# A graph layer with edge sums on one core: an eleventh range of counted edges, the close of node quads in bursts, and two banks for the last sums

## The reference, cut to what matters

```python
x = x + gnn(layernorm(x), src, dst, eps, W1, b1, W2, b2, gamma, beta)
x = x + ffn(layernorm(x)[None], gate_w, gate_b, w1, b1, w2, b2)[0]   # 8 experts, top 1

def gnn(h, src, dst, ...):
    neigh = segment_sum(h[src], dst)                 # 200000 rows of 256 values
    h = relu(((1 + eps) * h + neigh) @ W1 + b1) @ W2 + b2
    return (h - mean) * rsqrt(var + 1e-5) * gamma + beta   # mean, var over all nodes
```

## Time and profile before

| what | us |
|---|---|
| median of 3 runs (2704.42 to 2734.87) | 2713.54 |
| the profiled execution, whole | 2722.03 |
| its span, first to last instruction | 2720.3 |
| norm stage and plan, up to the first gather | 118.5 |
| groups 0 to 110 gathered | 118.5 to 1506.4 |
| groups 111 to 135 gathered | 1508.9 to 1844.3 |
| last sum, last two quads | to 1889 |
| routing and experts | 1891 to 2720 |

### The profile page before, as it was taken

How to read it: one execution, slowest core, us unless ns; L and a number is a source line. 1 busy time by engine, 2 the same in 40 slices (tenths; PEclk the granted TensorE clock), 3 DMA queues, 4 the chain that set the end, 5 groups by cost and what they waited for, 6 DMA issues and landing times. The chain is left out here.

```text
span 2720.3 us, 35963 instructions
## 1 busy us (share of the span) xinstructions
PE 1843.1 (68%) x9315; PEld 1055.5 (39%) x9316; DVE 1386.2 (51%) x4375; ACT 911.7 (34%) x1518; POOL 1553.5 (57%) x1530
## 2 busy tenths in 40 slices
PE   0035456767858878676787765557764888979996
PEld 0012223333424444333343433334332555646664
DVE  8834544545544443334342322223664676858886
ACT  6811012323323333223221110102553555545553
POOL 1266665665565666556565654650445566847775
PEclk9966678888779889889898877788887999989998
DMA  7653335656658766575677422421662322140220
GB/s 228 226 186 106 108 86 178 206 187 193 222 181 264 241 201 203 189 232 192 211 250 252 137 79 69 128 82 58 212 196 87 101 81 79 34 144 22 92 89 21
DMA packets 228639, 411.91 MB, mean 151 GB/s; under 512 B 46469, under 2 KB 110299, under 8 KB 228406
## 3 DMA queue, kind: packets, MB, share of 16 engines
q1 hardware_dynamic: 164742, 243.58, 27.4%
q0 software_dynamic: 61520, 164.41, 19.8%
q10 hardware_dynamic: 2144, 1.05, 0.1%
HBM read 338.06 MB, written 75.06 MB: 152 GB/s over the span
## 5 line engine op out<-in xcount | busy, mean ns | idle before, releaser
L948 POOL DMA_INDIRECT space<-table,space x1083 | 1036.6, 957 | 719.4 <-issue 310.2
L1043 PE MATMUL e_sums<-space 128*128 128x256 f16 x1728 | 258.3, 314 | 175.5 <-DVE space L1327 168.9
L2007 POOL TENSOR_TENSOR space<-space 128x512 f16<-128x512 f32 x200 | 296.8, 1510 | 105.3 <-ACT space L2141 100.8
L1316 DVE SCALAR_TENSOR_TENSOR space<-e_sums,above,space 128x256 f32 x141 | 68.2, 484 | 553.4 <-remote 391.5
L1043 PEld LDWEIGHTS e_sums<-space 128*128 128x128 f16 x1728 | 194.7, 113 | 239.4 <-issue 189.4
L1117 PE MATMUL e_up<-e_hT,edge_weights 128*128 128x512 f32 x384 | 211.9, 688 | 88.4 <-ACT e_hT L1218 57.3
L2097 PE MATMUL x_down<-space 128*128 128x256 f16 x2208 | 250.7, 276 | 15.9 <-DVE space L2234 15.6
L2073 PE MATMUL x_up<-space 128*128 128x512 f16 (+1 forms) x1200 | 253.1, 371 | 2.9 <-ACT space L2141 2.9
L1212 ACT ACTIVATE space<-e_tally 128x392 f32 (+1 forms) x193 | 104.9, 543 | 447.7 <-PE e_tally L1082 144.4
L2141 ACT ACTIVATE space<-x_up,b_two 128x512 f32<-128x512 f32 (+1 forms) x400 | 248.6, 691 | 17.3 <-PE x_up L2073 11.8
L1082 PE MATMUL e_tally<-w2f 128*128 128x490 f16 x343 | 136.3, 472 | 161.7 <-DVE w2f L1371 121.7
(11 more groups left out here) (230 smaller groups left out, 2522.3 us busy)
## 6 DMA issues: line engine op xcount, KB each, us to landing
w1f<-table SPq DMA_DIRECT2D x490, 256.0 KB
counts<-in_x SPq DMA_DIRECT2D x48, 512.0 KB, 4.6
space<-table,space POOLq DMA_INDIRECT x1083
slot_rows<-space SPq DMA_DIRECT2D x64, 268.0 KB
space<-slot_rows SPq DMA_DIRECT2D x32, 536.0 KB, 7.3
table<-space SPq DMA_DIRECT2D x25, 512.0 KB, 3.0
out<-space SPq DMA_DIRECT2D x24, 512.0 KB
w1f<-in_w SPq DMA_DIRECT2D x8, 1024.0 KB, 5.2
```

The source lines that it names most:

```text
L948: pool.indirect_dma_start(got[:, r, t, :], None, table.rearrange("p h d -> (p h) d"), bass.IndirectOffsetOnAxis(ap=idx[:, h, first + t:fir ...
L1043: ins = nc.tensor.matmul(sums[:, 0, 0:D], hot[:, place, t, :], got[:, r, t, half * D:(half + 1) * D], start=(t == 0 and half == 0), stop=( ...
L2007: nc.gpsimd.tensor_tensor(midl[:, j % 2, c, :], midf[:, c % MB, :], midh[:, j % 2, c, :], ALU.subtract).then_inc(s_mlo, 1)
```

## The change

It is one change of the plan with what that needs of memory.

- `UNITS` gets an eleventh range of 24 tiles: 504 counted tiles, so 133 gathered groups instead of 136. The windows of the groups from 108 on are 30 instead of 33. The tests of the plan hold for this `dst` as before.
- The range count is odd now, so `FILLED` is 0 and counting starts in slot 0 (before: slot 3). The group limits move with it.
- Until all ranges are spread, a slot gets one quarter (two if more than two quads wait, before: two or three). After that it gets four when a quad waits, else three. `CLOSE`, `TENSOR_ROOM` and `BACK` are moved to fit.
- `e_sums` has two banks, used in turn by the windows of the looped part. The second is also `product`, so all ranges must be spread before slot `SINGLE`. The sum of a window waits only for the add before the last one.
- Small tensors of the norm stage (`n_ok`, `n_first`, ...) lie in a free part of `counts`.

The planner then gives: tiles in slots 0 to 99, pieces in slots 20 to 106, the last spread in slot 107. 112 quarters lie in slots 0 to 107 and 80 from 108 on. Ten quads are turned from slot 108 on: in slots 108, 110, 112, 114, 116 and 118 (each with four quarters and then four, but for slot 118), then 121, 124, 127 and 131. 54 slots hold eight pieces, 2 of them without a quarter.

```diff
-UNITS = (152, 64, 50, 41, 36, 32, 29, 27, 26, 23)
+UNITS = (152, 64, 50, 41, 36, 32, 29, 27, 26, 24, 23)
-GROUPS = ((96, 4, 5), (168, 2, 5), (WIDE, 1, 5), (HT, 1, 7))
+GROUPS = ((96, 4, 5), (176, 2, 5), (WIDE, 1, 5), (HT, 1, 7))
-CLOSE = {3: 20, 4: 29, 5: 38, 6: 45, 7: 53, 8: 59, 9: 66, 10: 72, 11: 78, 12: 83, 13: 89, 14: 94, 15: 99, 16: 104,
-         17: 108, 18: 113, 19: 117, 20: 122, 21: 126, 22: 130, 23: 134}
-TENSOR_ROOM, VECTOR_ROOM, BEHIND = 1120, 960, 300
-BACK, LENT_FROM, LENT = 105, 18, QT * D * 13 // 2
+CLOSE = {3: 17, 4: 26, 5: 35, 6: 43, 7: 50, 8: 56, 9: 63, 10: 69, 11: 75, 12: 80, 13: 86, 14: 91, 15: 96, 16: 101,
+         17: 106, 18: 110, 19: 115, 20: 119, 21: 123, 22: 127, 23: 131}
+TENSOR_ROOM, VECTOR_ROOM, BEHIND = 1080, 960, 300
+BACK, LENT_FROM, LENT = 102, 18, QT * D * 13 // 2
...
-            n = H1C if slot >= NG - 1 else 3 if waiting or spread == NU or len(quarters) > 2 * (due - slot) else 2
+            n = H1C if slot >= NG - 1 or spread == NU and len(waiting) > 0 else 3 if spread == NU else 2 if len(waiting) > 2 else 1
...
-                    self.quarters[slot], quarters = [None, *quarters[:2]], quarters[2:]
+                    n = n if spread == NU and len(waiting) > 0 else min(n, 2)
+                    self.quarters[slot], quarters = [None, *quarters[:n]], quarters[n:]
...
-assert sorted(ORDER) == list(range(NQ)) and max(SLOTS_OF.spread) < NG - 2 and max(SLOTS_OF.turn) == NG - 2
+assert sorted(ORDER) == list(range(NQ)) and max(SLOTS_OF.spread) < SINGLE and max(SLOTS_OF.turn) == NG - 2
...
-        sums = psum("e_sums", [P, 1, 2 * D], F32)
+        sums = psum("e_sums", [P, 2, 2 * D], F32)
-        product = psum("e_product", [P, 2 * D], F32)[:, :]
+        product = sums[:, 1, :]
...
-                        pe.wait_ge(s_add, turn)
+                        pe.wait_ge(s_add, pe.snap(pe.snap(turn) - 1))
-                                ins = nc.tensor.matmul(sums[:, 0, 0:D], hot[:, place, t, :],
+                                ins = nc.tensor.matmul(sums[:, place, 0:D], hot[:, place, t, :],
...
-                            out=row, in0=sums[:, 0, 0:D], scalar=mask[:, group], in1=row,
+                            out=row, in0=sums[:, place, 0:D], scalar=mask[:, group], in1=row,
...
-                        add_window(group_no(dve.snap(last_group))).then_inc(s_add, 1)
+                        add_window(group_no(dve.snap(last_group)), dve.snap(1 - place)).then_inc(s_add, 1)
```

More of the change, by code:

```diff
@@ L694, in words @@
                 also(nc.vector.tensor_scalar(plan.cols[:, :], gmini, ok[:, 0:1], None, ALU.mult))
-                also(nc.vector.tensor_scalar(plan.above[:, :], blocki[:, 1, :], place[:, 0:1], 1.0 / X_SCALE, ALU.is_le,
+                also(nc.vector.tensor_scalar(plan.above[:, :], blocki[1], place[:, 0:1], 1.0 / X_SCALE, ALU.is_le,
                                              ALU.mult))
@@ L1310, in _, with add_window @@
                 flushed = [0]
-                def add_window(group):
+                def add_window(group, place=0):
                     for b, mask in ((0, plan.above), (1, plan.below)):
@@ L1443, in _ @@
                 dve.wait_ge(s_add, dve.snap(dve.snap(turn) - 1))
-                then(add_window(group_no(dve.snap(last_group))))
+                then(add_window(group_no(dve.snap(last_group)), dve.snap(dve.snap(dve.snap(turn) + 1) % 2)))
                 for slot in LATE:
```

33 lines of the change are left out of this document (17 added, 16 removed).

## The result

The change made the kernel slower. Its median is 2808.8 us (2783.7 to 2846.8) against 2721.8 (2704.4 to 2734.9) in the same comparison, a ratio of 1.029 with a 95% interval of 1.023 to 1.036. I had predicted 2689 us with a range of 2656 to 2722. The execution of 2846.8 us is in a slower state than the others and does not enter the ratio.

What follows compares the result with a forecast made beforehand. No engine is full; the limit is GpSimd's gather rhythm with waits for earlier sums. The terms -36.9 + 0 + 0.5 + 13.7 - 2 give -24.7 us, 2689 us against the median of 2713.5; range 2656 to 2722.

Steps and rivals of the forecast that it cites:

- the eleventh range on TensorE: Slots 0 to 107: 49 us of added matmuls hidden by the gather rhythm; 0, ends -29 and +8 us.
- the rival of the pieces: Early slots with eight pieces: two more long gaps behind table loads, +16 us, 2705 us; chance 0.17.
- The even plan: Early part and turns: fewer overfull slots save 20 us, packed pairs are seldom held, 7 more; 2662 us; chance 0.22.
- Three groups less: Late part: 24 gathers and three slots go, at the bare pace of 12.3 us each; -36.9 us.
- the late one: Sign of being right: the late part from group 111 to 132 takes 285 to 320 us.
- the early one: Sign of being right: group 3 to 110 takes 1330 to 1360 us.
- The denser end: From slot 108 on: longer packed pairs of slots +6.5 us, more held turns +7.2; +13.7 us, ends 0 and +74.
- The end bound by TensorE: From slot 108 on: further turns held at 9.65 us each; 2749 us with all ten held; chance 0.15.
- One-hots: VectorE: 15 us more of one-hots, hidden in idle time but slowing the gathers slightly; +0.5 us.
- Two banks: Last windows: TensorE no longer waits for the add before; -2 us, ends -7 and 0.
- The clock: Late packed pairs: by the clock rule fuller slots stay warm, making the sum 4.5 us lower.
- bare group: Gather rhythm: eight gathers and a gap of 2.5 to 2.7 us, 12.3 us from group to group.

Runs made afterwards that it cites:

- experiment 14: The changed kernel as it is, run again on another chip of the 2700 us kind: 2814.7 us, 1.033 of the kernel before.
- experiment 2: The kernel before with all pieces and then all tiles of a slot in one share, on a 2300 us kind of chip: 2502.6 us, ratio 1.089.
- shares kept: The changed kernel with pieces and tiles handed out in three shares in every slot: 2705.9 us, 0.995 of the kernel before, on a 2700 us kind of chip.
- seven pieces: The changed kernel with three shares in every slot and at most seven pieces a slot instead of eight: 2695.1 us, ratio 0.990, on a 2700 us kind of chip.
- experiment 7: The changed kernel with three shares in every slot and one bank for the last sums: 2341.4 us, ratio 1.018, on a 2300 us kind of chip.

## Why the prediction was wrong

**The group numbers.** The prediction's pace has a slip: 848 gathers are 106 groups, so the stretch in the earlier trace rows ends with the first gather of group 109, and that at 1508.92 belongs to group 110 (so in the table of times, too, the first stretch is groups 0 to 109 and the second 110 to 135). The pace before was 1345.32 / 106 = 12.69 us early and 331.92 / 25 = 13.28 late, an excess over 12.3 of 41 and 24 us instead of 29 and 37. It shifts weight from the late to the early part and would have moved the sum by little.

**The failed step is "the eleventh range on TensorE: 0, ends -29 and +8".** It measured +110.8 us in the profiled execution, and +138 in that of experiment 14 (1495.7 - 1357.6). I wrote that "13 quarters leave the same slots" and that "the new plan is more even", and in the rival of the pieces that "the quarter in nearly every one of these slots now covers a load". I priced the quarters that move as TensorE time alone. But the number of quarters in a slot is also the number of shares into which its pieces and tiles are cut. One quarter where there were none or two turned three or two shares into one. This could be read before any run, from `parts_of` and `share` and from the plan's 44 such slots. The trace of before could not show it: its one slot with eight pieces and one part (slot 102) has no tiles, so that there is nothing to alternate. It kept the next group 18.7 us away, against 13.4 behind the other 37 slots of eight pieces, but four slots of the old plan with three parts kept it 19.9 to 21.2 us away, and on the chip of experiment 2 slot 102 took 11.0. With the shares kept the step measured 1370.1 - 1357.6 = +12.5 us, some 13 more by the median of that kernel, and with seven pieces -3.7. So as a price of the range alone, on this kind of chip, 0 and the upper end of +8 were somewhat low; on the other kind the range costs 54.5 us or more.

**The rival of the pieces** (2705 us, +16) had the right place, full slots whose sums come late behind table loads, and named the sign that came true: more than five gaps over 8 us, of which there are 12. Its price was a seventh of what happened, since it counted more full slots of the old kind and not slots of a new kind. **The even plan** (2662) did not occur as the change was written; the seven pieces version is nearest to it, 28.8 us under before where this rival had 51.5.

**Three groups less: -36.9** was right to a few us. Of the signs I had named, the late one was missed narrowly (285 to 320 us; it was 283.6, and 273.6 if the first gather is taken at group 111 as counted here) and the early one by far (1330 to 1360; it was 1468.4). The late part from the first gather of group 110 to that of the last group went from 331.9 us in 25 groups to 283.6 in 22, which is 48.3 us; at the old late pace three groups are 39.8. On the faster kind of chip the whole late stretch won 31.9, for 3 x 10.0.

**The denser end: +13.7** had the wrong sign in this execution: the 49.6 us that the late part won are 11.5 more than three groups at 12.3 us and the 1.2 us of the banks. Of ten turns from slot 108 on, two were held, for 9.3 and 11.3 us from transposes to products (in slots 116 and 121), not 3.75. The hold of the earlier trace rows is there, and the same turn can be held in one kernel and go through in another. That this depends on where it falls against the gathers, as the prediction said, fits but was not tested:

```profile
1514.33 1.06 PE L1109 MATMUL e_up<-ident,space 128*128 128x128 f32 x8 [2.36 <-remote]
1525.01 5.24 PE L1120 MATMUL e_up<-e_hT,edge_weights 128*128 128x512 f32 x6 [9.61 <-issue]
```

This is slot 108 of the kernel with seven pieces, held for 10.7 us; in the changed kernel the same turn took 2.2. The stretch from group 110 to the last add took 305 to 341 us over ten executions with the same late plan on this kind of chip, with up to four turns over 10 us. The longest of them, 340.5, belongs to four such turns, the shortest, 304.7, has none. So the term's size, 7.2 us for holds, is within what varies from one early part to the next, and +6.5 for the pairs is not to be seen: the turns that are not held take 2.2 to 3.1 us, most of them less than the 3.05 that I had put in. **The end bound by TensorE** (2749) was a rival on the right side of the result for the wrong reason: the end won 49.6 us.

**One-hots: +0.5.** A gather took 961 instead of 957 ns, which is 4 x 857 = 3.4 us for the early part. The Trainium skill (SBUF — State Buffer, the part on the port pair that VectorE and GpSimd share) says that fast VectorE copies lock GpSimd out while they run; by that rule the whole 15 us of one-hots could have been added, as an estimate, and the trace shows 3.4.

**Two banks: -2** fits in sign and nearly in size. From the last gather's end to the last add it was 24.9 us before and 23.7 after. The rows of TensorE that answer to the earlier trace rows show the wait for the add gone, and a shorter one for the next one-hots in its place:

```profile
1918.71 2.83 PE L1063 MATMUL e_sums<-space 128*128 128x256 f16 x16 [3.05 <-DVE space L1353]
1922.04 2.35 PE L1063 MATMUL e_sums<-space 128*128 128x256 f16 x16 [0.49 <-DVE space L1353]
```

L1353 makes one-hots, L1318 adds; the first of the two waits is longer than any before, and it is why the gain is small. With one bank experiment 7 showed no difference either.

**The clock.** In the three lumped slots the granted clock is 0.74, in the same slots with three shares 1.00, and that is 13 us of longer matmuls in 57. I had weighed the clock for the late part only, at 4.5 us. In slot 56 above it is 1.00, which is 2.4 GHz, from 888.8 to 895.5 us, where TensorE is busy for 4.79 us and has the wait of 1.83, and 0.50, which is 1.2 GHz, from 895.6 to 909.1, where it is busy for 11.03 us, before it rises again. The Trainium skill (TensorE: Matmul & The Clock Gate, Part 1) says that the array runs at 1.2 GHz after idle time and at 2.4 GHz once it has been busy; the trace agrees with these two changes.

In sum: on this kind of chip the change with shares kept (2705.9 against 2723.9, or -18; by the ratio -13) would have been within the range around the forecast of -24.7 us, which for its size is luck in part: the late part won more than its terms and the early part lost what they had at 0. The change as written added about 109 us to that (2814.7 - 2705.9).

## What to carry to other kernels

Where a helper cuts work by the length of a list, changing the list for any other reason changes the cut. When a diff changes how many items of one kind go into a step, read the functions that use this count, also those that the diff leaves alone. A step of before that already has the new count is a hint only if it also has the work that the count divides; here the one such slot had no tiles. Work that waits on a handshake of banks and work that waits on a ring of loads should alternate: in a block each shows its waits, and the matmuls around them ran slower, which here was the larger part of the price. The gain of a saved iteration is to be held against the pace of the chip that runs it.

## What the runs showed of the hardware

**Two kinds of chip.** I had not expected that the same kernel takes 2298 us on one chip and 2722 on another. The gathers take the same time on both (0.95 us, 1.25 apart). What differs is when a finished sum is seen while they run. The kernel before on the chip of the prediction, GpSimd's gathers, TensorE's sum and VectorE's add:

```profile
875.30 1.91 PE L1043 MATMUL e_sums<-space 128*128 128x256 f16 x16
876.33 0.94 POOL L948 DMA_INDIRECT space<-table,space  x1 [0.30 <-issue]
877.58 0.95 POOL L948 DMA_INDIRECT space<-table,space  x1 [0.30 <-issue]
880.60 0.48 DVE L1316 SCALAR_TENSOR_TENSOR space<-e_sums,above,space 128x256 f32 x1 [4.23 <-remote]
...
881.18 0.95 POOL L948 DMA_INDIRECT space<-table,space  x1 [2.66 <-remote]
```

And the kernel before with three shares on a chip of the other kind:

```profile
877.61 1.91 PE L1044 MATMUL e_sums<-space 128*128 128x256 f16 x16
877.94 0.94 POOL L949 DMA_INDIRECT space<-table,space  x1 [0.30 <-issue]
879.19 0.95 POOL L949 DMA_INDIRECT space<-table,space  x1 [0.30 <-issue]
879.70 0.48 DVE L1317 SCALAR_TENSOR_TENSOR space<-e_sums,above,space 128x256 f32 x1 [0.65 <-PE e_sums L1044]
...
880.44 0.95 POOL L949 DMA_INDIRECT space<-table,space  x1 [0.30 <-issue]
```

In the first the sum ends at 877.21, the eighth gather at 878.53, and the add starts at 880.60: 3.4 us after the sum and 2.1 after the gather. In the second the sum ends at 879.52 and the add starts 0.18 us later, in the middle of the gathers. Over slots 4 to 107, of 66 sums that ended while gathers ran 60 were seen more than 1.2 us late in the first, at the median 1.9 us after the eighth gather's end; in the second 10 of 92 were, and the median delay is 0.18 us. That is the gap of 2.6 us between groups, which I had taken as a fixed part of the bare group. The hold of the turns is probably the same thing; the rows show only that it occurs on the same kind of chip. From group 3 to the last add the kernel before takes 1717.9 us on the one kind and with three shares 1372.6 on the other, which is 345 of the 409 us between the two spans. No turn from slot 108 on was held on the faster kind. What holds the signals there the rows don't say.

**A load's pace and the lump.** With loads of half the size the lumped slots keep the next group 14.03 us away instead of 15.78 and 16.18, and the interleaved ones 12.99 and 13.13 instead of 13.50. The 14.03 is of the execution that is 28 us under its median. So the size of the loads matters in a lump (1 to 2 us a slot) and less where pieces and tiles alternate (0.4 us).
